# Edge stage of a graph kernel: PE's three signals given by drain instructions behind the matmuls

## The reference

```python
e = edge_feats @ W_e + b_e
m = relu(e + node_feats[src])
agg = segment_sum(m, dst)
h = agg + (1.0 + eps) * node_feats
z = relu(batchnorm(h @ W1 + b1)) @ W2 + b2
x = layernorm(x + z)
for W, b in layers:                      # three
    hw = h @ W
    h = relu(segment_sum(hw[src] * norm, dst) + b)
x = layernorm(x + h)
```

## Time and profile before

| | us |
|---|---|
| Median of 3 runs (3533.81 to 3544.42) | 3540.62 |
| Profiled execution, its own time | 3530.44 |
| Its span, first to last instruction | 3528.6 |
| PE busy | 2950.6 (84%) |
| DVE busy | 1946.3 (55%) |
| POOL busy | 1615.7 (46%) |
| ACT busy | 1527.0 (43%) |
| Mean granted clock of TensorE, share of 2.4 GHz | 0.854 |

### The profile page before, as it was taken

The page is one execution under the profiler, slowest core; times in us unless marked ns, Lnnn a source line. Parts: engine busy times, 40 slices in busy tenths (PEclk is TensorE's granted clock), DMA queues, the critical chain, the costliest instruction groups (busy, mean ns, idle before and its releaser), DMA issues.

```text
span 3528.6 us, 56408 instructions
## 1 busy us (share of the span) xinstructions
PE 2950.6 (84%) x17477; PEld 2191.8 (62%) x17477; DVE 1946.3 (55%) x3284; ACT 1527.0 (43%) x2341; POOL 1615.7 (46%) x1582
## 2 busy tenths in 40 slices
PE   3878888878788778878788888888799999999995
PEld 2555555555555555555555555555688888888885
DVE  5555555555555555555555555555678873335335
ACT  1434444444434444444444444444655554445442
POOL 6666666666666666666666666663000000000000
PEclk8877788887877887778888877878899999999998
DMA  5433443343434433334443443432323333333332
GB/s 178 109 97 104 108 109 107 106 109 107 106 105 105 109 108 107 105 105 109 107 106 106 109 107 106 108 107 75 104 106 117 139 125 122 128 134 135 123 128 92
DMA packets 201844, 394.77 MB, mean 112 GB/s; under 512 B 43068, under 2 KB 156519, under 8 KB 196183
## 3 DMA queue, kind: packets, MB, share of 16 engines
q1 hardware_dynamic: 149720, 277.89, 23.4%
q0 software_dynamic: 50176, 102.50, 12.6%
q10 hardware_dynamic: 1662, 10.71, 0.8%
HBM read 286.13 MB, written 104.80 MB: 111 GB/s over the span
## 4 chain that ended last, share of the span: by engine, by line
PE 55%; DVE 19%; another core or an unknown queue 15%; issue 8%; ACT 1%; POOL 1%; DVEq 0%; DMA 0%; ACTq 0%; POOLq 0%
PE psA L822 15%; PE psE L930 12%; PE psA L930 11%; DVE z L1079 8%; PE psE L792 6%; PE psS L806 5%; DVE work L1059 3%; DVE z L1071 3%; DVE onehot L1065 2%; PE psS L809 2%; POOL work L629 1%; DVE acc L1083 1%; PE psA L901 1%; PE psA L941 1%
## 5 line engine op out<-in xcount | busy, mean ns | idle before, releaser
L629 POOL DMA_INDIRECT work<-in_x_flat,idx x1568 | 1608.2, 1026 | 807.6 <-issue 422.3
L668 ACT ACTIVATE work<-psA 128x490 uint8 x1568 | 819.0, 579 | 1420.0 <-remote 831.9
L822 PE MATMUL psA<-z 128*128 128x490 bf16 x3136 | 1086.1, 477 | 107.5 <-issue 106.7
L1059 DVE TENSOR_TENSOR work<-psE,work 128x1024 f32<-128x1024 f32 x196 | 240.1, 1225 | 1075.4 <-remote 1045.0
L1079 DVE TENSOR_SCALAR z<-iota_c,key 128x980 bf16<-128x980 f16 x1568 | 681.3, 495 | 21.2 <-PE psA L822 0.5
L792 PEld LDWEIGHTS psE<-we,work 65*128 65x128 f32 x3136 | 521.2, 220 | 150.1 <-issue 92.5
L792 PE MATMUL psE<-we,work 65*128 65x128 f32 x3136 | 511.8, 301 | 29.4 <-issue 26.1
L822 PEld LDWEIGHTS psA<-z 128*128 128x128 bf16 x3136 | 242.8, 111 | 355.7 <-issue 299.7
L806 PE MATMUL psS<-onehot,work 128*128 128x72 f32 x3136 | 395.0, 278 | 73.3 <-issue 71.8
L930 PE MATMUL psE<-wide,halves 128*128 128x500 f32 (+1 forms) x2058 | 448.8, 376 | 5.6 <-ACT halves L745 5.4
L806 PEld LDWEIGHTS psS<-onehot,work 128*128 128x128 f32 x3136 | 375.6, 195 | 88.2 <-issue 86.4
(11 more groups left out here) (157 smaller groups left out, 1277.2 us busy)
## 6 DMA issues: line engine op xcount, KB each, us to landing
counts<-adjacency SPq DMA_DIRECT2D x36, 3062.5 KB, 9.8
adjacency<-work SPq DMA_DIRECT2D x784, 122.5 KB
work<-in_edge_cols SPq DMA_DIRECT2D x196, 256.0 KB
work<-in_x_flat,idx POOLq DMA_INDIRECT x1568
counts<-adjacency SPq DMA_DIRECT2D x3, 1531.2 KB, 6.1
acc<-in_x_cols ACTq DMA_DIRECT2D x1, 3136.0 KB, 22.9
xn<-in_x_rows ACTq DMA_DIRECT2D x1, 3136.0 KB, 30.3
x_spill<-xn SPq DMA_DIRECT2D x12, 256.0 KB, 2.3
```

What stands on the lines that cost most here:

```text
L629: gp.indirect_dma_start(gath[0:size(g), g % R, j, :], None, x_flat[:, :], bass.IndirectOffsetOnAxis(ap=idx[0:size(g), g, j:j + 1], axis=0) ...
L668: act.activation(full[:, p % SLOTS, HC * i:HC * i + HC], ring[:, bass.ds(at, HC)], ACT.Copy).then_inc(evac_ok, 1)
L822: mm = pe.matmul(ring[:, bass.ds(at, HC)], weights, hot[:, k % RB, HC * half:HC * half + HC], start=(k < 1), stop=True, skip_group_check=( ...
L1059: ve.tensor_tensor(gath[0:n, g % R, :, :], psE0[0:n, :, :], gath[0:n, g % R, :, :], ALU.add).then_inc(sum_ok, 1)
```

## The change

In the edge stage, each of the three signals of PE was an increment on the last matmul of its group. Now a drain instruction stands behind that matmul and carries the increment. There are 196 drains for `edge_mm`, 196 for `win_mm` and 784 for `chunk_mm`. The matmuls, their order, the values of the semaphores and all waits stay.

```diff
@@ edge_product @@
                 if j1 == J:
-                    mm.then_inc(edge_mm, 1)
+                    pe.drain().then_inc(edge_mm, 1)
@@ window @@
                 for j in range(J):
                     mm = pe.matmul(psS[:, W:2 * W], ones_b[0:n, :], high[:, j, :, 1], start=(j == 0), stop=(j == J - 1))
-                mm.then_inc(win_mm, 1)
+                pe.drain().then_inc(win_mm, 1)
@@ chunk_pair @@
                         mm = pe.matmul(ring[:, bass.ds(at, HC)], weights, hot[:, k % RB, HC * half:HC * half + HC],
                                        start=(k < 1), stop=True, skip_group_check=(k >= 1))
-                mm.then_inc(chunk_mm, 1)
+                pe.drain().then_inc(chunk_mm, 1)
```

## The result

The changed kernel takes 5076.81 us (median of 4 runs, 5074.12 to 5077.46) beside 3541.0 us for the kernel before on the same chip: ratio 1.434, interval 1.4315 to 1.4364. The forecast was 3870 with a range of 3600 to 4340. The direction was right, the size was not: the loss is 1536 us where 340 were forecast.

A forecast was written before the change was run, and what follows sets the result against it. TensorE was taken to bound the edge stage at 12.25 us a step, GpSimd the floor below. Work of 9.65 us plus 4.35 of bubbles made 14.0; over 196 steps +340 us on 3530.44 gave 3870, range 3600 to 4340.

The forecast's parts named there:

- The restart: Pause after each drain behind window and chunk pairs until PE's next matmul starts; 1.04 us a step in sum.
- The loads: Two register loads from the table behind the edge product's drain, no longer hidden by queued matmuls: 2.2 us a step.
- The issue idle at line 809: TensorE's idle time called "issue", largest before line 809, was assumed to vanish with the drains: 2.34 us a step.
- the first rival: The stall in PE's issue stays because instructions reach PE too slowly: 2.3 us more a step, 4320 us, chance 0.13.
- the third rival: Edge stage's clock rises as even, short pauses keep TensorE at 2.4 GHz: 3450 us if fully reached, chance 0.07.
- the last rival: The drain does not hold PE's stream, only signals come earlier: 3160 us or no change, chance 0.08.
- I take off 0.04: Edge stage's granted clock falls from 0.80 to 0.76 as TensorE gets less busy: 9.65 us of work a step.
- tails: Ends of the last matmuls that no longer overlap the next work at each drain: six of 0.17, 1.0 us a step.
- the clock falls: Rival: edge stage's clock drops to 0.6 because the array pauses every few matmuls: 4330 us, chance 0.07.
- the floor below TensorE: GpSimd's gathers and the time between them need 10.3 us a step, taken as the next bound after TensorE.
- my bubbles without tails: Idle PE time added per edge step by restarts (1.04), slower register-fed first matmuls (0.1) and table loads (2.2 us).
- late signals: PE's pair and edge signals arriving over 5 us after their matmuls, read as tied to register loads with matmuls in flight.

The follow-up runs named there:

- e7: Changed kernel with PE's table loads for the next step moved ahead of the edge product's drain: 4696.59 us, ratio 1.338 to the kernel before.
- e4: Changed kernel with the signals back on the matmuls and a bare drain without signal behind each: 5047.38 us, ratio 1.441 to the kernel before.
- e17: Kernel before with fixed rows loaded by SyncE instead of gathers, and drains behind the window and the four chunk pairs: 4285.53 us, ratio 1.305.
- e18: Kernel before without gathers (fixed rows), drains behind four chunk pairs and edge product, table loads ahead of the edge drain: 3263.8 us, ratio 0.995.
- e6: Changed kernel with GpSimd's gathers replaced by one SyncE load of fixed rows a step: 4671.11 us, ratio 1.331 to the kernel before.
- e5: Kernel before, without drains, with GpSimd's gathers replaced by one SyncE load of fixed rows a step: 3010.32 us, ratio 0.858.
- e1: Kernel before with only the edge product's signal given by a drain, one a step: 4622.34 us, ratio 1.319.
- e15: Changed kernel without gathers (fixed rows), all six drains, table loads ahead of the edge drain: 4156.54 us, ratio 1.176 to the kernel before.

## Why the prediction was wrong

**The idle terms held.** The restart was put at 0.30 us behind window and first pair, 0.20 behind the second, 0.12 behind the others; measured are 0.33, 0.32, 0.23 and, behind the third, 0.07. The loads were put at 2.2; measured are 2.05 in the timeline, and 1.74 of idle time by e7. The issue idle at line 809 went altogether, as assumed, so the first rival falls as it was told, with instructions that reach PE too slowly; what had caused that idle stayed (below). The clock did not rise, so the third rival falls. The drain holds the stream, so the last rival falls too: e4.

**The step that failed first is the clock**, "I take off 0.04 ... and get 0.76: ... 9.65 us of work". Measured is 0.54. With tails, 9.65 + 1.0 = 10.65 us of work were forecast and 15.26 are measured: 4.61 us more, 904 us of busy time in 196 steps. My own bound for all matmuls at 1.2 GHz, 14.05 + 1.0, is met within 0.2. The step's reason was rows 1, two stages of which the less busy has the lower clock. Two rows don't make a law. The busy share came out as I put it, 75% forecast and 76% measured, and the clock did not follow: e17 is busy 92% at 0.54, e18 84% at 0.95. I also had the mechanism as a rival ("the clock falls"), but priced it at 0.6 and gave it 0.07, with "most pauses are 0.3 us or less" against it. That is what e17 refutes: short pauses suffice, if they stand in the wrong place. The Trainium skill (TensorE: Matmul & The Clock Gate, Part 1) says that the clock follows how busy TensorE has been of late. At the grain of these rows busy share and clock run opposite in e17 and e18; whether the rule holds at a finer one no run here shows.

**The second step that failed is the path through GpSimd**, for which the sum has no term. I had GpSimd as "the floor below TensorE", with "2 us of slack a step, more in a longer step". It has none: its gathers begin with the window's signal, and PE's completions come free about 1.7 us behind the eighth. My last sentence named "drains of several microseconds" as what would prove me wrong, and they came, behind the fourth pair. After has 4.91 us idle, my bubbles without tails came to 3.35: 1.56 us more, 306 us. e6 takes the gathers away and 1.76 us of idle go.

As a count this closes: 3870 + 904 + 306 = 5080, measured 5077. It is not the price of each. With the hold gone and the clock low (e6) the step is 18.18 us. With the hold in place and all at 2.4 GHz I estimate 17.2, from the loop of 20.1 less 1.0 for the edge product (2.07, and 1.05 in rows 3) and 1.9 for the window (4.14, and 2.25 in the step of e5 from 1008 us); no run has this. Either alone misses the forecast 14.0, by 4.2 and by 3.2 us; both together miss it by 6.2.

**The cause of the late signals was misread.** I tied them to register loads with matmuls in flight. e5 has those loads and no late signals. They go with the gathers: 3010 us beside 3509. The word "remote" stood beside GpSimd too, which I passed over. So TensorE's "issue" idle was not its own, and the step before was the loop's, not TensorE's. It mattered, since PE worked on beside late completions before, and a drain makes PE itself wait for them: e1, whose edge drain takes 6.5 us.

In the prediction I set the Trainium skill's rule (PSUM — Partial Sum Buffer, "Engine vs sequencer instructions"), that an update attached to a matmul fires when it completes, against the trace. Without gathers the traces agree with it: in e5 every wait of VectorE for the edge product ends with its matmul. With the gathers the signal comes microseconds after the matmul, and the drain waits for the same late completion.

Two slips in the working change nothing: 0.45 us in rows 3 is the distance from chunk to chunk, not from pair to pair, and half of line 809's slow value of 0.49 is 0.25, not 0.27.

## What to carry to other kernels

Before a drain goes into TensorE's stream, ask what its completions wait for: here it met the same late completions that the signal had, and took from TensorE the work that it had done beside the delay. Follow the engine that the signal starts, too: if its work comes back to your own wait, the two make a loop, and it has no slack. Price each pause twice, as its own hole and as what the granted clock makes of all matmuls around it, and try each place alone and together: 0.33 us behind the window cost nothing alone and, with the gathers left out, some 950 us beside the pair drains. Do not infer the clock from the busy share.

## What was not expected of the hardware

- Matmul completions arrive late while GpSimd runs its indirect gathers. In the steps above the held drains end about 1.7 us after the eighth gather, in the changed kernel and in e1; with the gathers gone the longest pair drain falls from 4.9 to 2.1 us, and the kernel before from 3509 to 3010. That it is the gathers is shown; by which path they hold PE's completions is not.
- TensorE stayed nearly always at 1.2 GHz (0.54) while busy 92%, with holes of 0.33 us and less in the step shown (e17), and at 2.4 GHz nearly all the time while busy 84% (e18).
- The granted clock at the start of the stage can be wrong. In e15 it reads 1.00 from 100 to 300 us, while line 806 (809 there) takes 3.66 us at 205, as it does at 601, where the clock reads 0.50. In the changed kernel it reads 1.00 from 100 to 145 us, while line 806 takes 3.66 us at 110 and 130: the first slices of its page (9 and 7) are too high.
- The kernel before took 3502, 3509, 3538 and 3541 us in four comparisons, and 3282 and 3283 in two, on other chips. The changed kernel was run only beside the slower figure.
